# Attention softmax of a fused block: later turn and spread for the last head, earlier spread and subtractions for the first

## The reference

```python
q = rms_norm((x @ wq).reshape(B, 256, 16, 128), q_norm_w)       # 16 query heads, 256 tokens
k, k_ctx = rms_norm(x @ wk), rms_norm(h_ctx_kv @ wk_ctx)          # 4 key/value heads
k_full = concat([k_ctx, k]); v_full = concat([v_ctx, v])          # 4096 context + 256 own keys
scores = einsum('blhd,bmhd->bhlm', q, k_full) / sqrt(128) + mask  # causal on the own 256
probs = softmax(scores, axis=-1)
out = einsum('bhlm,bmhd->blhd', probs, v_full).reshape(B, 256, 2048) @ wo
```

## Time and profile before

| what | value |
| --- | --- |
| median of 3 runs | 988.67 us (988.24 to 989.04) |
| profiled execution, device time | 988.25 us |
| its span | 986.5 us |
| busy: PE, DVE, ACT, POOL | 98%, 79%, 62%, 57% of the span |
| attention loop (first L600 to last weigh) | about 234 to 692 us |
| granted TensorE clock, mean | 0.998 of full speed |

### The profile page before, as it was taken

How to read it: one execution, slowest core, us unless ns; L and a number is a source line. 1 busy time by engine, 2 the same in 40 slices (tenths; PEclk the granted TensorE clock), 3 DMA queues, 4 the chain that set the end, 5 groups by cost and what they waited for, 6 DMA issues and landing times.

```text
span 986.5 us, 15792 instructions
## 1 busy us (share of the span) xinstructions
PE 971.4 (98%) x5695; PEld 856.5 (87%) x5695; DVE 776.1 (79%) x1179; ACT 612.3 (62%) x1026; POOL 560.7 (57%) x517
## 2 busy tenths in 40 slices
PE   9999999999999999999999999997999999999998
PEld 8888888889899999999999999976788988888887
DVE  6654667545988888888888988999698877777775
ACT  5443344336767777677776677682498566666663
POOL 4643444331499999999999999996001132222222
PEclk9999999999999999999999999999999999999999
DMA  7557654566304130222105041310700785555540
GB/s 293 182 167 249 214 184 135 171 214 226 117 1 133 50 107 2 86 97 58 50 13 170 28 146 49 118 54 1 278 21 1 282 292 204 187 181 184 188 160 22
DMA packets 56525, 131.10 MB, mean 133 GB/s; under 512 B 4192, under 2 KB 36352, under 8 KB 55424
## 3 DMA queue, kind: packets, MB, share of 16 engines
q1 hardware_dynamic: 56448, 130.09, 38.9%
HBM read 101.21 MB, written 28.87 MB: 132 GB/s over the span
## 4 chain that ended last, share of the span: by engine, by line
PE 91%; DVE 4%; POOL 2%; issue 1%; ACT 1%; DMA 1%; SPq 0%; DVEq 0%; POOLq 0%
PE bank L526 18%; PE bank L600 17%; PE bank L629 17%; PE bank L508 13%; PE bank L928 9%; PE bank L930 5%; PE bank L736 1%; PE bank L535 1%; PE bank L623 1%; POOL first_max L1926 1%; PE bank L625 1%; PE bank L627 1%; DVE weights L1122 1%; DVE first_max L1088 1%; PE bank L792 1%
## 5 line engine op out<-in xcount | busy, mean ns | idle before, releaser
L600 PE MATMUL bank<-qT_hi,kT 128*128 128x256 f32 (+1 forms) x1088 | 295.2, 345 | 0.6 <-ACT weights L1631 0.6
L1926 POOL TENSOR_TENSOR first_max<-first_max,weights 128x512 f32<-128x512 f32 x214 | 278.9, 1303 | 20.7 <-PE bank L629 0.4
L629 PE MATMUL bank<-weights,vN 128*128 128x256 f32 (+1 forms) x896 | 258.4, 375 | 0.0
L1631 ACT COPY weights<-bank 128x512 f32<-128x512 f32 (+1 forms) x272 | 154.8, 580 | 99.9 <-PE bank L600 58.0
L600 PEld LDWEIGHTS bank<-qT_hi,kT 128*128 128x128 f32 x1088 | 196.1, 189 | 19.4 <-ACT weights L1631 1.2
L1096 DVE TENSOR_TENSOR first_max<-bank,first_max 128x512 f32<-128x512 f32 x196 | 134.9, 688 | 35.1 <-ACT weights L1631 29.8
L1122 DVE TENSOR_TENSOR weights<-weights,bank 128x1024 f32<-128x1024 f32 x128 | 155.0, 1211 | 1.8 <-PE bank L656 1.8
L600 PE MATMUL bank<-qT_lo,kT 128*128 128x256 f32 (+1 forms) x544 | 153.6, 282 | 0.0
L1635 ACT ACTIVATE weights<-weights 128x1024 f32<-128x1024 f32 x144 | 144.5, 1003 | 10.5 <-DVE weights L1122 9.5
L526 PE MATMUL bank<-w_ctx_hi,ctx_hl 128*128 128x512 f32 x512 | 144.7, 394 | 0.3 <-ACT w_ctx_hi L1594 0.3
L629 PEld LDWEIGHTS bank<-weights,vN 128*128 128x128 f32 x896 | 141.5, 189 | 3.0
(11 more groups left out here) (262 smaller groups left out, 1730.1 us busy)
## 6 DMA issues: line engine op xcount, KB each, us to landing
e_raw<-in_experts SPq DMA_DIRECT2D x51, 768.0 KB, 4.4
k_spill<-k_stage SPq DMA_DIRECT2D x16, 1024.0 KB, 5.5
kT<-k_spill SPq DMA_DIRECT2D x15, 1024.0 KB, 5.2
v_spill<-v_stage SPq DMA_DIRECT2D x16, 512.0 KB, 6.8
vN<-v_spill SPq DMA_DIRECT2D x16, 512.0 KB, 3.5
ctx_raw<-in_ctx SPq DMA_DIRECT2D x15, 512.0 KB, 4.2
w_raw<-in_w_qkv SPq DMA_DIRECT2D x6, 1024.0 KB, 5.1
comb<-c_spill SPq DMA_DIRECT2D x8, 512.0 KB, 6.0
```

Source lines behind the costliest of these rows:

```text
L600: done = e.matmul(dst, kT[:, w, kt * P:(kt + 1) * P], qT[a][:, h, q0:L], start=m == 0, stop=m == 2)
L629: done = e.matmul(dst[:, q0:L], vN[:, kt, :], weights[:, cols], start=kt == 0, stop=kt == KTILES - 1)
L1631: e.copy(s_buf[h % 2][:, g, 0:width(g)], bank[SCORE_BANKS[s % len(SCORE_BANKS)]][:, 0:width(g)]).then_inc(taken, 1)
L1926: e.tensor_tensor(run_sum[:, :], run_sum[:, :], here, ALU.add).then_inc(summed, 1)
```

## The change

It changes six numbers in two lines. For head 0 the reduce goes from step 19 to 18, the spread from behind score 24 to behind score 23, and its nine subtractions stand two steps sooner in DVE's program, each ahead of two maxima that it followed before. For head 15 the turn goes from step 274 to 275, the reduce from 275 to 276, the spread from 275 to 277.

```diff
-TURN_AT, REDUCE_AT, SPREAD_AT = (5, 5, 4, 2), (2, 5, 5, 3), (7, 7, 6, 3)
+TURN_AT, REDUCE_AT, SPREAD_AT = (5, 5, 4, 3), (1, 5, 5, 4), (6, 7, 6, 5)
 FINISH_AT = (10, 2)
-SOONER = 2
+SOONER = 4
```

## The result

| kernel | median | lowest, highest | runs |
| --- | --- | --- | --- |
| before | 988.60 us | 987.72, 989.82 | 20 |
| changed | 990.61 us | 987.93, 993.08 | 20 |

The ratio is 1.0018 with a 95% interval of 1.0012 to 1.0025: 1.8 us slower (2.0 by the medians), just inside the 0.2% that the prediction called no change, and three times the +0.6 us that it forecast. The median is 0.2 us above the upper end of the range, 990.4. The profiled execution took 990.23 us, with a span of 988.5.

The account below looks back on a forecast made before the run. It took POOL's chain to bound the attention stage, with PE's gains covered by it. 988.25 us profiled + 0.61 (first head) + 0 (last head) = 988.9, as a median of runs 989.3; range 987.4 to 990.4.

Parts of the forecast that it names:

- called no change: Whole kernel: time within 0.2%, 2 us, of the kernel before; chance 0.81.
- the signs by which it said it would be wrong: Score 39 before 274.5, no POOL wait at 287, or a second stretch of granted clock at 0.5.
- First subtraction 0.96 sooner, POOL's start 0.96 sooner: First head's start: first subtraction at 253.25 and POOL's first p_lo at 259.16, each 0.96 us sooner.
- PE's 0.32 wait: First head, PE at 257.04: score 29's wait for the bank that ACT copies late goes, 0.32 us.
- Maximum of step 35 0.96 later, score 39 at +24.16: First head's end: DVE's maximum L1092 0.96 us later, score 39 at 275.50, PE's 0.30 wait becomes 2.2.
- POOL's lead lost in one wait for the second head's cast: Second head's group 2: cast 0.96 us late, slack 0.35, so POOL starts p_lo 0.61 later, as does the end.
- Last head worth 0: Last head's spread: 1.75 us saved on PE, then lost waiting for POOL, at `outT` of head 13; worth 0.
- The clock: Rival at score 39: new wait brings 3.4 us at half speed, costing up to 1.7, total 991.0; chance 0.07.
- by the nearer row (1.75) it costs nothing, and that the sum takes: Score 39: PE stayed at 2.4 GHz after a 1.75 us wait, so the new 2.2 us wait adds no clock cost.

Follow-up runs that it names:

- first head alone: The first follow-up: only the first head's part of the change, last head's turn, reduce and spread as in the kernel before; 990.86 us, 1.0017 on the kernel before.
- fourth experiment: Changed kernel with the first head's ninth subtraction put back behind the maximum of step 35; 990.95 us, 1.0011 on the kernel before.
- third experiment: Changed kernel with 14 matmuls of 128 columns, result unread, on PE ahead of score 39; 990.53 us, 1.0017 on the kernel before.
- ninth experiment: Changed kernel with 9 matmuls of 128 columns, result unread, on PE ahead of score 39; 989.42 us, 1.0014 on the kernel before.
- twelfth: The changed kernel itself, measured again on the third chip; 990.58 us, 1.0020 on the kernel before.
- last head alone: Only the last head's part of the change, first head as in the kernel before; 989.11 us, 1.0002 on the kernel before.

## Why the prediction held, and where it did not

It called no change, and the 1.8 us lie just inside the 2 us that it allowed for that; with three times the loss it forecast, this is in part luck. Of the signs by which it said it would be wrong, one came true: the granted clock shows a second stretch at 0.5.

- *First subtraction 0.96 sooner, POOL's start 0.96 sooner.* Right: +1.91 for +2.87, and POOL's first p_lo at 258.70 is +7.83 for +8.78. PE's 0.32 wait went, and the one for p_lo ends at +9.16 (I had +9.14).
- *Maximum of step 35 0.96 later, score 39 at +24.16.* The mechanism is right, the size was off: 1.26 later, +24.46. The 0.30 is L1080, which adds the causal mask. It took 0.63 before and 0.91 now. These are its rows and those of the sum on POOL beside it, before and then changed:

```profile
269.43 1.30 POOL L1926 TENSOR_TENSOR first_max<-first_max,weights 128x512 f32<-128x512 f32 x1
270.52 0.63 DVE L1080 TENSOR_TENSOR weights<-weights,causal 128x384 f32<-128x384 f32 x1
```

```profile
270.84 1.28 POOL L1926 TENSOR_TENSOR first_max<-first_max,weights 128x512 f32<-128x512 f32 x1
271.62 0.91 DVE L1080 TENSOR_TENSOR weights<-weights,causal 128x384 f32<-128x384 f32 x1
```

POOL's sum ended 0.21 after L1080 began before, and 0.50 after it now; L1080 ended 0.42 and 0.41 after POOL's sum. In all fourteen profiles this last number is 0.40 to 0.42, whatever L1080's own length (0.58 to 0.91). The Trainium skill (SBUF — State Buffer, Who interferes with whom) says that a DVE instruction with two SBUF inputs contends with a GpSimd one that reads SBUF, and the later one blocks; the trace agrees in this place, with 0.28 us. So an instruction moved by 1.1 us against the other engine gets another length.
- *POOL's lead lost in one wait for the second head's cast.* Right, and in the trace without a fall of the clock almost to the number: wait 1.79 (I had 1.6), start 0.84 late (0.61, and 0.30 from L1080 would be 0.91). POOL's chain then ran on to the end but for the one gap of 0.4.
- *Last head worth 0.* Right within the noise: 1.0002. The 1.75 us went into waits for POOL, only not all at `outT`.
- *The clock.* Here the prediction failed. Its step was "by the nearer row (1.75) it costs nothing, and that the sum takes", and the chance of 0.07 that went with it. The wait of 2.50 us was followed by 3.4 us at 1.2 GHz in two of the three profiles that have it (the changed kernel twice; not the first head alone), and so was the 2.15 us of the fourth experiment. The nearer row was no guide: in the third experiment's profile a stretch at half speed follows a wait of 1.56 us. The mean clocks bound how often: the 6 of 20 runs at 0.998 have one stretch only, and in every profile with the 4.5 us wait that one is at the end, so it fell at score 39 in at most 14. Filling the wait was worth 1.2 us of the 2.0. The same wait had the stretch at 275.7 in one execution, at 278.2 in another, in a third none. The Trainium skill (TensorE: Matmul & The Clock Gate, Part 1) says that activity releases the throttle and that the point varies from run to run; the traces agree with the second, as far as three executions go. The fall deserved a term in the sum: a chance times 1.7.

Sum of the parts by the medians of the third chip: order 989.42 - 988.54 = 0.9, clock 990.58 - 989.42 = 1.2, last head 0, in all 2.0. The order is shown by the traces of the first and ninth experiment and by the ninth's runs; the clock by those traces against the changed kernel's, and by the difference of the ninth and twelfth. What decides in a run whether the clock falls in a wait of 2.5 us isn't settled.

## What to carry to other kernels

In an order written out by hand, work that is moved ahead pushes other work of the same engine back by as much; list what is pushed, find the first that another engine waits for, and move only what has nobody behind it: all nine subtractions early gave +1.8 us, seven early and the last two behind the maximum that PE waits for gave -1.2. Ask of an engine that never waits (POOL here) where its chain starts and ends: two sums taken from it, with the clock that this kept up, were worth more than every shift of steps. And price a new wait of TensorE at more than its length: here a stretch at half speed followed 4.5 us of waiting in nine of nine profiles, waits of 2.15 to 2.50 us in three of four, and one of 1.56 us near the start of the program, but not one of 1.65 there, nor any of the six of 1.2 to 1.9 us at the last spread. Each stretch moves a single run by up to 1.7 us.

## What I had not expected of the hardware

- Filling a wait of TensorE with matmuls whose result nobody reads made the kernel 1.5 us faster (988.54 to 987.09); the clock stayed at 1.00 where it was 0.50 for 3.4 us in the kernel before. In the profile of the last head alone it was 0.50 over a window of 6.7 us.
- A float32 matmul of 128 by 128 columns took 0.23 to 0.24 us of PE in a row of them, as two records each (18 records in 2.17 us for nine), twice what I had reckoned.
- One engine's instruction can set the length of another's: L1080 on DVE ended 0.40 to 0.42 us after the end of POOL's sum in fourteen profiles of fourteen.
- The kernel before has groups as well: on the three chips its runs at 0.998 averaged 988.1 to 988.8 and those at 0.997 988.9 to 989.6.
